# A conv-attention-FFN kernel on one core: tokens of x turned on VectorE instead of TensorE, and one LayerNorm group moved in the order

## The reference, cut to what matters

```python
# per image; C = 256 channels, N = 1024 tokens
xn  = group_norm(x, norm_w, norm_b)              # 8 groups of 32 channels
q, k, v = split(qkv_w @ xn + qkv_b)
a   = softmax(q.T @ k / 16)                      # 1024 x 1024
x   = x + proj_w @ (v @ a.T) + proj_b            # first residual, needs x by tokens
t   = x.T                                        # tokens x channels
l   = layer_norm(t)
u   = l / |l|
t   = t + softmax((u @ u.T) ** 2) @ l            # second attention, symmetric scores
l   = layer_norm(t)
w   = sign(W - mean(W)) * mean(|W|)
y   = l @ w + bias
t   = t + round(7 * clip(y, -1, 1)) / 7
out = t.T                                        # back to channels x pixels
```

## Time and profile before

| | |
|---|---|
| median of 3 runs | 1794.2 us (1793.78 to 1795.09) |
| the profiled execution, its own time | 1793.89 us |
| its span | 1792.2 us |
| TensorE clock granted, mean | 0.998 of full speed |
| PE busy | 97% of the span |
| DVE busy | 76% |
| ACT busy | 52% |
| POOL busy | 39% |
| DMA queue of SP, share of 16 engines | 26.8% |

### The profile page before, as it was taken

The page is one execution under the profiler, slowest core; times in us unless marked ns, Lnnn a source line. Parts: engine busy times, 40 slices in busy tenths (PEclk is TensorE's granted clock), DMA queues, the critical chain, the costliest instruction groups (busy, mean ns, idle before and its releaser), DMA issues.

```text
span 1792.2 us, 34184 instructions
## 1 busy us (share of the span) xinstructions
PE 1743.2 (97%) x11938; PEld 1603.0 (89%) x11938; DVE 1358.4 (76%) x2564; ACT 936.0 (52%) x1444; POOL 695.7 (39%) x1174
## 2 busy tenths in 40 slices
PE   7999999999999999999999999999999999999997
PEld 6898988989889998899989999899898988999887
DVE  6778777787777877778787787877778777787675
ACT  3645546455463654735547364564645546455462
POOL 0442616326152361614516144261532615336151
PEclk9999999999999999999999999999999999999999
DMA  3405124050330504205041150412404123050230
GB/s 123 122 24 153 36 82 129 23 168 20 105 106 23 187 0 128 83 35 176 0 149 61 59 152 7 153 51 72 139 23 154 33 92 118 23 186 2 95 94 24
DMA packets 97054, 152.88 MB, mean 85 GB/s; under 512 B 11648, under 2 KB 70400, under 8 KB 97024
## 3 DMA queue, kind: packets, MB, share of 16 engines
q1 hardware_dynamic: 97024, 152.48, 26.8%
HBM read 76.95 MB, written 75.50 MB: 85 GB/s over the span
## 4 chain that ended last, share of the span: by engine, by line
PE 88%; ACT 4%; DVE 3%; issue 2%; DMA 2%; POOL 1%; SPq 0%; ACTq 0%; POOLq 0%; DVEq 0%
PE wide L373 32%; PE wide L475 6%; PE narrow L475 6%; PE narrow L477 6%; PE wide L477 6%; PE wide L476 6%; PE narrow L476 6%; PE narrow L373 5%; PE turn L584 3%; PE turn L545 2%; PE narrow L515 2%; PE turn L575 2%; PE turn L428 2%; PE turn L592 1%; ACT ln_x L769 1%
## 5 line engine op out<-in xcount | busy, mean ns | idle before, releaser
L373 PE MATMUL wide<-xn_hi,prob 128*128 128x512 f32 x1024 | 303.4, 398 | 0.0
L786 ACT ACTIVATE ln<-tok,ln_shift,ln_r 128x256 f32<-128x256 f32 x128 | 68.4, 593 | 298.0 <-POOL ln_shift L1275 298.0
L373 PEld LDWEIGHTS wide<-xn_hi,prob 128*128 128x128 f32 x1024 | 185.4, 188 | 38.4
L1270 POOL TENSOR_TENSOR ln_v<-ln_mv,ln_eps 128x2 f32<-128x2 f32 (+1 forms) x112 | 22.1, 198 | 475.8 <-DVE ln_mv L1077 240.6
L755 ACT ACTIVATE prob<-e_back 128x1024 fp32r<-128x1024 f32 x112 | 118.3, 1056 | 141.8 <-DMA e_back<-e_scratch 141.7
L1317 POOL TENSOR_TENSOR carrier_p<-ones 128x1 f32<-128x1 f32 x60 | 11.7, 195 | 436.8 <-DVE y_sb L1087 434.3
L748 ACT ACTIVATE expo<-wide,neg_max 128x1024 f32<-128x1024 f32 x128 | 142.4, 1113 | 70.3 <-DVE neg_max L1007 70.0
L1014 DVE STREAM_TRANSPOSE x_norm<-expo 128x1024 f32<-128x1024 f32 x112 | 139.2, 1243 | 45.2 <-ACT expo L748 44.8
L1007 DVE TENSOR_REDUCE neg_max<-wide 128x1 f32<-128x1024 f32 x128 | 155.6, 1215 | 15.7 <-PE wide L373 15.2
L1307 POOL TENSOR_TENSOR prob<-expo,prob 128x128 fp32r<-128x128 f32 (+6 forms) x112 | 143.2, 1290 | 54.1 <-DVE prob L1051 54.1
L373 PE MATMUL wide<-xn_lo,prob 128*128 128x512 f32 x512 | 160.7, 394 | 0.0
(11 more groups left out here) (179 smaller groups left out, 5456.3 us busy)
## 6 DMA issues: line engine op xcount, KB each, us to landing
e_scratch<-x_norm SPq DMA_DIRECT2D x112, 512.0 KB, 3.0
e_back<-e_scratch SPq DMA_DIRECT2D x448, 128.0 KB, 3.1
x_raw<-in_x SPq DMA_DIRECT2D x32, 512.0 KB, 3.8
out<-y_sb SPq DMA_DIRECT2D x32, 512.0 KB, 3.6
tok<-in_L_conv_qkv_w SPq DMA_DIRECT2D x1, 768.0 KB, 6.2
ln<-in_L_conv_proj_w SPq DMA_DIRECT2D x1, 256.0 KB, 6.7
ln<-in_L_ffn_weight SPq DMA_DIRECT2D x1, 256.0 KB, 4.2
out_bias<-in_L_conv_proj_b SPq DMA_DIRECT2D x1, 128.0 KB, 3.8
```

What stands on the lines that cost most here:

```text
L373: mm = pe.matmul(o, lhsT, r, start=first and i == 0, stop=last and i == len(parts) - 1)
L786: act.activation(ln2[:, n], tok[:, n], ACT.Identity, bias=ln2_shift[:, n:n + 1], scale=ln2_r[:, n:n + 1]).then_inc(ln2_made, 1)
```

## The change

What it does, in four parts:

1. x comes into the kernel a second time, by `load_quads`: four DMAs of 256 KB per image, in runs of 1 KB, into `e_back` (the memory into which the turned exponentials come later). Partition group q (32 partitions) gets the tokens of quarter q of the image; within it a partition is one of 32 channels. POOL adds the projection's bias there (`bias_quads`, two instructions of 128x1024 per image, in `back` behind `norm_lo` and ahead of the second LayerNorm's coefficients). DVE turns it in 32x32 blocks from `e_back` straight into `x_tok` (`x_tokens`, two instructions). PE's 16 turns per image are gone. For this a tile of 128 tokens now has 32 tokens of each quarter of the image instead of 128 neighbours.
2. So the other places that touch the token order read or write it in pieces of 32: `normalise` on ACT, `ffn_out` on ACT, `output` on DVE (now two instructions instead of one for each half), and the store, now two DMAs of 256 KB per half in runs of 512 bytes.
3. The waits follow: `x_raw` may be reloaded as soon as it is normalised; the quads wait for the last `e_back` of the image to be consumed; the first two fetches wait for `x_tokens`. DVE's order is now `query_lo(b, 0)`, `x_tokens(b, 0)`, `query_lo(b, 1)`, `x_tokens(b, 1)`.
4. In the second attention, ACT writes the LayerNorm rows of tiles 6 and 7 (`layer_norm1(b, 3)`) ahead of `exp2(b, 3)`, and their copy to `val` (`value_rows(b, 3)`) only behind `cosT_hi(b, 3)`; PE does `turn_e2(b, 3)` ahead of `turn_cos(b, 3)`; POOL does `e2_lo(b, 4)` ahead of `value_lo(b, 3)`.

```diff
 # SP
             def store(f, hf):
                 sp.wait_ge(out_made, 2 * f + hf + 1)
-                sp.dma_start(out_d[f, :, :, hf * HALF:(hf + 1) * HALF], y_sb[:, hf]).then_inc(stored[hf], 16)
+                for k in range(KC):
+                    sp.dma_start(out_quad_d[f, k, :, :, hf * P:(hf + 1) * P],
+                                 y_sb[:, hf, k].rearrange("p (q f) -> p q f", q=SQ)).then_inc(stored[hf], 16)
+
+            def load_quads(b):
+                for q in range(SQ):
+                    sp.dma_start(x_quad[q * Q:(q + 1) * Q], x_quad_d[b, q]).then_inc(quad_loaded, 16)
...
             def reload(b):
-                sp.wait_ge(xT_up, 2 * b)
                 sp.wait_ge(xn_made, 2 * b)
                 load_x(b)
+
+            def reload_quads(b):
+                sp.wait_ge(eT_made[0], 16 * (SENT_OF[0] * b + 1))
+                load_quads(b)
...
                 sp.wait_ge(e1_written[n % 2], due)
-                sp.wait_ge(eT_made[n % 2], due)
+                if n < 2:
+                    sp.wait_ge(quad_turned[n], due)
+                else:
+                    sp.wait_ge(eT_made[n % 2], due)
...
                 front(b, b - 1)
+                reload_quads(b + 1)
 # PE, front
-                for k in range(KC):
-                    pe.wait_ge(x_loaded[k], 16 * b + 16)
-                if f is not None:
-                    pe.wait_ge(pT_made, (NT - 1) * f + NT - 1)
-                x_by_tokens(b, 0)
                 if f is not None:
                     pe.wait_ge(t2_made, NT * f + NT - 1)
                 queries(b, 0)
-                x_by_tokens(b, 1)
...
                 scores2(b, 4)
+                turn_e2(b, 3)
                 turn_cos(b, 3)
-                turn_e2(b, 3)
                 scores2(b, 5)
 # ACT
-                act.activation(x_norm[:, k], x_raw[:, k], ACT.Identity, bias=gn_b[:, k:k + 1],
+                act.activation(by_tile(x_norm[:, k]), by_quad(x_raw[:, k]), ACT.Identity, bias=gn_b[:, k:k + 1],
                                scale=gn_a[:, k:k + 1]).then_inc(xn_made, 1)
...
-                    act.activation(y_sb[:, hf, m], places["y"][hf][m], ACT.Identity,
+                    act.activation(by_quad(y_sb[:, hf, m]), by_tile(places["y"][hf][m]), ACT.Identity,
...
                 cosT_hi(b, 2)
+                layer_norm1(b, 3)
                 exp2(b, 3)
-                layer_norm1(b, 3)
                 unit_rows(b, 3)
                 exp2(b, 4)
                 cosT_hi(b, 3)
+                value_rows(b, 3)
                 exp2(b, 5)
 # DVE
             def x_tokens(b, g):
-                dve.wait_ge(xT_up, 2 * b + g + 1)
-                dve.tensor_tensor(x_tok[:, HT * g:HT * (g + 1), :],
-                                  turn[:, :].rearrange("p (t c) -> p t c", t=HT),
-                                  out_bias[:, :].unsqueeze(1).broadcast_to([P, HT, C]), ALU.add).then_inc(xT_made, 1)
+                dve.wait_ge(quad_biased, 2 * b + g + 1)
+                dve.transpose(x_tok[:, :, g * P:(g + 1) * P].rearrange("p n (cb cc) -> p cb n cc", cc=Q),
+                              e_back[:, g].rearrange("p i (n t) -> p i n t", n=NT)
+                              ).then_inc(quad_turned[g], 16 * SENT_OF[g])
...
-                dve.tensor_tensor(y_sb[:, hf], places["tT"][hf][:, :].rearrange("p (k t) -> p k t", k=KC), y_sb[:, hf],
-                                  ALU.add).then_inc(out_made, 1)
+                for k in range(KC):
+                    y = by_quad(y_sb[:, hf, k])
+                    last = dve.tensor_tensor(y, by_tile(places["tT"][hf][:, k * HALF:(k + 1) * HALF]), y, ALU.add)
+                last.then_inc(out_made, 1)
...
-                x_tokens(b, 0)
...
                 query_lo(b, 0)
+                if f is None:
+                    dve.wait_ge(prep_act, 2)
+                x_tokens(b, 0)
+                query_lo(b, 1)
                 x_tokens(b, 1)
-                query_lo(b, 1)
                 value_lo(b, 0)
 # POOL
+            def bias_quads(b, g):
+                pool.wait_ge(quad_loaded, 16 * SQ * (b + 1))
+                pool.tensor_tensor(e_back[:, g], e_back[:, g],
+                                   quad_bias[:, SQ * g:SQ * (g + 1), 0:1].broadcast_to([P, SQ, NT * Q]),
+                                   ALU.add).then_inc(quad_biased, 1)
...
                 e2_lo(b, 3)
+                e2_lo(b, 4)
                 value_lo(b, 3)
-                e2_lo(b, 4)
...
                     for k in range(KC):
                         norm_lo(b + 1, k)
+                    for g in range(2):
+                        bias_quads(b + 1, g)
                 for g in range(N2):
                     layer_norm2(b, g)
```

More of the change, by code:

```diff
@@ L68, in build @@
     x_d = x.rearrange("b (k p) h w -> b p k (h w)", p=P)
-    out_d = out.rearrange("b (k p) h w -> b p k (h w)", p=P)
+    x_quad_d = x.rearrange("b (cb cc) (q h) w -> b q cc cb (h w)", cc=Q, q=P // Q)
+    out_quad_d = out.rearrange("b (k p) (q h) w -> b k p q (h w)", p=P, q=P // Q)
     with ExitStack() as ctx:
@@ L97, in build @@
         out_bias = sb("out_bias", [P, C])
+        quad_bias = sb("quad_bias", [P, C // Q, Q])
         norm_w_c = sb("norm_w_c", [P, KC])
@@ L131, in build @@
         e_back = sb("e_back", [P, 2, SQ, NT * Q])
+        x_quad = e_back[:, :, :, :].rearrange("p s i f -> p (s i) f")
         e_scratch = nc.dram_tensor("e_scratch", (NT, P, N), F32).ap()
@@ L209, in build @@
         xn_lo_made = sem("xn_lo_made")
-        xT_up = sem("xT_up")
-        xT_made = sem("xT_made")
+        quad_bias_made = sem("quad_bias_made")
+        quad_loaded = sem("quad_loaded")
+        quad_biased = sem("quad_biased")
+        quad_turned = [sem("quad_turned0"), sem("quad_turned1")]
         a_up = sem("a_up")
@@ L285, in tile, with by_tile, by_quad @@
             return slice(t * P, (t + 1) * P)
+        def by_tile(a):
+            return a.rearrange("p (n q t) -> p q n t", q=SQ, t=Q)
+        def by_quad(a):
+            return a.rearrange("p (q n t) -> p q n t", q=SQ, t=Q)
         def offset(J):
@@ L356, in _ @@
             front(0, None)
+            reload_quads(1)
             with sp.Fori(1, B - 1) as b:
@@ L362, in _ @@
             store(B - 1, 1)
-            sp.wait_ge(stored[0], 16 * B)
-            sp.wait_ge(stored[1], 16 * B)
+            sp.wait_ge(stored[0], 16 * KC * B)
+            sp.wait_ge(stored[1], 16 * KC * B)
         @block.tensor
@@ L421, in group_vars @@
                           ).then_inc(gn_var_up, 1)
[L423 to L426, removed]
-                    for k in range(KC):
-                        mm = pe.transpose(turn[:, t * C + k * P:t * C + (k + 1) * P],
-                                          x_raw[:, k, tile(HT * g + t)], ident[:, :])
-                mm.then_inc(xT_up, 1)
             def queries(b, m):
@@ L618, in front @@
                 if f is not None:
-                    pe.wait_ge(xT_made, 2 * b + 2)
                     turn_ln2(f, 0)
@@ L656, in front @@
                     pe.wait_ge(out_made, 2 * f + 2)
-                else:
-                    pe.wait_ge(xT_made, 2 * b + 2)
                 turn_last_e1(b)
@@ L770, in layer_norm1, with value_rows @@
                                    scale=ln_r[:, n:n + 1]).then_inc(ln1_made, 1)
+            def value_rows(b, g):
+                n0, n1 = GROUPS1[g]
                 act.wait_ge(ln1_made, NT * b + n1)
@@ L851, in front @@
                 layer_norm1(b, 0)
+                value_rows(b, 0)
                 exp1(b, 6)
@@ L862, in front @@
                 layer_norm1(b, 1)
+                value_rows(b, 1)
                 unit_rows(b, 1)
@@ L865, in front @@
                 layer_norm1(b, 2)
+                value_rows(b, 2)
                 unit_rows(b, 2)
@@ L1033, in residual1 @@
                 dve.wait_ge(t1_steps, i + 1)
+                if n == 0:
+                    for g in range(2):
+                        dve.wait_ge(quad_turned[g], 16 * SENT_OF[g] * (b + 1))
                 dve.scalar_tensor_tensor(tok[:, n], out1[n][:, 0:C], inv_sum1[:, n:n + 1], x_tok[:, n],
@@ L1364, in _ @@
             gn_coefficients(0)
+            pool.wait_ge(quad_bias_made, 1)
+            for g in range(2):
+                bias_quads(0, g)
             front(0, None, True)
```

6 lines of the change are left out of this document (4 added, 2 removed).

## The result

The changed kernel takes 1765.66 us (median of four runs, 1764.46 to 1766.2), the kernel before 1794.64 beside it: a ratio of 0.9837, 95% interval 0.982 to 0.9854. The forecast was 1765. The profiled execution has a span of 1764.5 us against 1792.2.

What follows compares the result with a forecast made beforehand. PE, busy 97% of the span, was taken as the bound. Turns of x 20.0 us (15 x 1.29 + 0.65) plus second attention 9.6 (16 x 0.6), less 0.8 for the tail: 28.8 off 1793.89, so 1765; range 1747 to 1782.

Steps and rivals of the forecast that it cites:

- Part 1: Without PE's turns of x, scores1(b, 0) starts sooner, held only by the second query_lo on DVE: 1.29 us less per image.
- Part 2's gain: Second attention, LayerNorm rows ahead of exp2(b, 3), turn_e2(b, 3) ahead of turn_cos: PE's wait shrinks 1.05 us per image.
- Its give-back: At product2(b, 0), PE waits 0.43 us per image for DVE's e2_last_lo, made late through POOL.
- The bias in `back`: POOL's two bias_quads take 4.94 us, covered with some 3 us to spare before the second LayerNorm's coefficients.
- rival C: In back, POOL keeps DVE out, residual2 is late, PE stalls: 1793 us (chance 0.05) or 1809 and the like (0.06).
- The tail: The last store becomes two issues instead of one, with four times the runs: 0.8 us more.
- Image 0: The first image's front gains half the loop's saving from the turns of x, 0.65 us, plus 0.6 in second attention.
- A: The second attention's reordering gives nothing, as lateness on POOL and DVE eats it: 1775 us, chance 0.14.
- D: Quads or stores still move when the fetches need the queue: one us per image, 1781 us, chance 0.05.
- B: No PE wait at scores1(b, 0) or product2(b, 0), DVE and POOL being in time: 50 us less, 1745, chance 0.1.

Runs made afterwards that it cites:

- the three together: The changed kernel with both x_tokens ahead of query_lo(b, 0) from image 1, value_lo(b, 3) ahead of e2_lo(b, 4), image 0's bias behind the signs: 1749.94 us.

## Why the prediction was right

**Part 1** was right to a tenth of a microsecond where it happens: `scores1(b, 0)` was put 8.85 us after the product's end and came at 8.74, that is 1.40 us gained, and 1.29 behind the slower first matmuls. The forecast had 1.29 without them, so that the two numbers are the same is chance. The two `query_lo` on DVE and the turn between them are the cause, by the run with both turns first. What the working lacked is that 0.10 us go again at the first `turn_cos`, where LayerNorm's chain through POOL and ACT does not come as much sooner as PE; the profile shows the loss, and the cause is argued, since no run took it apart.

**Part 2's gain** was forecast at 1.05 us, and scores2(b, 5) gained 1.08. **Its give-back** was put at 0.43, by DVE's `e2_last_lo`; it is 0.36, and the step was half right. The working carried the delay to `e2_last_lo` through the copy in front of it, which waited out POOL's subtraction. In the trace that copy gets in ahead of it (0.41 us), and `e2_last_lo` itself is held, for 2.50 us, until 0.55 us behind the end of `e2_lo(b, 6)`. POOL's own `e2_lo(b, 6)` is late for PE as well, one token block sooner, which the working did not look at. The cause behind both was named rightly, `value_lo(b, 3)` ahead of `e2_lo(b, 5)`. Alone the part is worth 0.79 net (0.6 forecast).

**The bias in `back`** was to be covered, and was, with the room that the forecast gave it. Its price was too high: 2 x 2.47 against 4.22 for both:

```profile
859.94 4.95 POOL L1289 TENSOR_TENSOR xn_lo<-x_norm,xn_hi 128x1024 fp32r<-128x1024 f32 x2 [0.99 <-ACT xn_hi L742]
...
864.85 4.22 POOL L1338 TENSOR_TENSOR e_back<-e_back,quad_bias 128x1024 f32<-128x1024 f32 x2
...
872.79 0.20 POOL L1296 TENSOR_TENSOR ln_v<-ln_mv,ln_eps 128x4 f32<-128x4 f32 x1 [3.72 <-DVE ln_mv L1098]
```

```profile
862.67 2.77 DVE L1077 TENSOR_TENSOR prob<-expo,prob 128x512 fp32r<-128x512 f32 x1
...
865.55 0.48 DVE L1093 SCALAR_TENSOR_TENSOR tok<-narrow,inv_sum,tok 128x256 f32<-128x256 f32 x1
```

This is also the answer to rival C, and to the earlier trace rows. `norm_lo` ends at 864.89, DVE's `e2_last_lo`, held for 2.77 us, gets in there and ends at 865.44, and the first bias shares that stretch with it; `residual2` starts to write its tile at 865.55, as if nothing had been added. POOL did not go on over DVE's head, and the run with the bias twice shows no cost either. In it, the first bias takes 2.35 us and the three others 1.90: the 0.45 is DVE's turn.

**The tail** was put at 0.8 us and is 0.7. The last stores on SP's queue, the answer to the earlier trace rows, are four now:

```profile
1754.67 7.05 SPq L320 DMA_DIRECT2D out<-y_sb  x4
```

**Image 0** is the term that was mis-sized, and its sign was wrong: 0.65 + 0.6 us of gain forecast, 1.66 of loss in the profile. The working took half of the loop's saving and did not look at what DVE and POOL do there at the same time. Putting the bias and the two turns of image 0 elsewhere gives 3.2 us back. Up to `scores1(0, 0)` the front of image 0, whose turns of x are gone as well, became 0.4 us longer (10.59 against 10.19). Some of the rest is not shown to be the change's. The first product of the preparation, which waits for the loads, started anywhere from 9.33 to 11.05 us in the ten profiles of this study, before 9.41, after 10.83, and within the changed kernel's own variants over the whole of that range. So 1.4 us of the 1.66 are within what one execution differs from another. Only two of the ten profiles are without the quads (9.41 and 9.71), so it stays open whether their load has a part in it.

These errors partly cancel: against the forecast, 14 x (1.99 - 1.89) = 1.4 us more in the loop, 2.9 less in image 0, and 0.4 more in the rest (1.5 measured, 1.89 - 0.8 = 1.1 forecast). That the forecast lies within 1 us of the median is luck in that much; the terms of the loop, which carry the gain, are not.

**The rivals:** A and C were refuted by runs. D was so for the stores; for the quads there is the profile alone, in which no wait of PE for the fetched blocks appears in the loop. B was wrong for the change as it was forecast. Its mechanism is half real: neither give-back need come, but only after more edits (the three together are 44.7 us below before, where B had 50).

## What to carry to other kernels

When work leaves the engine that bounds the kernel, what is late next can depend on the order of the engine that takes the work over, as here on VectorE and on GpSimd. Put the moved work into that engine's hole, ahead of the instructions that others wait for: the same two turns cost 6.6 us in one place more than in the other. Walk every stage for it, the one-time start too: the largest error here came from the image that was not looked at.

## What the runs showed of the hardware that was not expected

- POOL's addition of the bias (one operand repeated over 256 elements, fp32 out) took 1.90 us for 128x1024 where DVE did not get in between; its subtraction of two full operands (`norm_lo`, fp32r out) 2.47 on average. Which of the differences makes it shorter was not tried.
- A wait of PE that ends within 0.03 us of the time at which the next matmul was due still costs: 0.08 or 0.09 us ahead of the matmul and 0.10 behind it, 0.18 for each of the two blocks in `product2(b, 0)`; the run with GpSimd's order as before has neither wait, and its period is 0.35 us shorter.
- DVE, held up by a running instruction of POOL, got in at the next boundary between two of POOL's: `norm_lo` ends at 864.89, DVE's subtraction at 865.44, and of POOL's next two instructions, alike in form, the first took 2.36 us and the second 1.90. In image 0 the first comparison of the signs got in at such a boundary too, at 23.02; the second had to wait for the end of POOL's last addition, at 25.07.
- The four stores of an image in runs of 512 bytes took 2.82 us of SP's queue from the first's start to the last's end, the two of before 1.06.
